# A scratch copy of w1 in bf16, and w2 loaded behind the first FFN1 stretch

## The chip, the cores and the metric

One Trainium2 chip, all 8 cores. Every core runs the same program on its own 2048 rows of x (with 128 rows of neighbours on either side), and holds all weights. The time is that of the slowest core, in microseconds (us). Before the change it is 1194.36 us, the median of 2 runs (1194.09 and 1194.64).

## What is computed

The input is x of shape (4, 4096, 1024). It is normalised per row, goes through an attention whose weights are fixed Gaussians, and beside it through a feed-forward net; both results are added to x.

```python
xn = _layernorm(x, axis=-1)
# attention: 8 heads of 128 columns
v = xn @ input_weights.T
attended = einsum('hqk,bhkd->bhqd', gaussian_probs, v)
att = attended @ output_weight.T
# feed-forward: w1 is 1024 x 4096, w2 is 4096 x 1024
h = relu(einsum('bsd,dw->bsw', xn, w1) + b1)
ffn = einsum('bsw,wd->bsd', h, w2) + b2
return x + att + ffn
```

The Gaussians are narrow (a deviation of at most 8 rows), so a block of 128 rows needs three blocks of v.

## The kernel before

The program is written out instruction by instruction for five engines through a small class, `Emitter`. `op` appends an instruction to one engine's list, with the events it waits for, and returns an event: a semaphore and a value. The DMAs of GpSimd all raise the semaphore `w` by 16, those of SyncE raise `x` and `o`. Since DMAs of one semaphore can land out of order, `op` groups them: GpSimd may issue `BATCH` = 4 DMAs, then the next one first waits until all those so far have landed (a drain), and the event of each DMA in a group gets the count of the whole group as its value. So whoever waits for one DMA of a group waits for all of it.

In order of the program:

- *Start.* SyncE loads b1, b2 and the identity. GpSimd loads win (L158), wout (L161) and w2 in four quarters (L166); all are f32 in HBM and are cast to bf16 by the DMA. VectorE and ScalarE make the 24 blocks of Gaussian weights (`probsT`; L193 writes each). Then TensorE transposes win and wout in 128 blocks (L206), and VectorE copies them out of PSUM (L211).
- *Half H = 0 and 1*, each 1024 rows of the result. Layer norm of 10 tiles of 128 rows, mostly on VectorE, with 8 transposes a tile on TensorE (L283). The product with win, 160 matmuls (L308). The Gaussian blocks, 192 small matmuls (L333).
- *Quarter Q = 0 and 1 of each half*, 512 rows. FFN1: 32 chunks `wc` of 128 columns of w1. GpSimd loads a chunk into one of four buffers `w1b` (L361), TensorE does 8 matmuls of 128x512 (L373), ScalarE applies bias and relu and writes h (L381). A buffer is free again when the matmuls of the chunk four earlier are done. Two neighbouring chunks, an even and the odd one behind it, share a PSUM tile, and the odd one waits for the relu of the even one. FFN2 (L418): 4 tiles, each 16 matmuls with wout and 64 with w2 into one PSUM tile; VectorE adds x and b2 (L423, L425); SyncE stores. The first matmul of every tile waits for all relus and for the last load of w2.

So FFN1 comes four times, and w1 is read from HBM in f32 each time, in rows of 128 elements (512 B), 1024 such rows a chunk. `w1b` holds four chunks of 256 KB.

The order on GpSimd is that of the source: win, wout, four quarters of w2, then the chunks of w1, 32 in each of four stretches. With six DMAs ahead of the chunks, a group begins at chunk 2, 6, 10 and so on, and the group that begins at chunk 30 takes in chunks 0 and 1 of the next stretch.

## Time and profile before

| what | us |
|---|---|
| median of 2 runs | 1194.36 |
| profiled execution, its own time | 1198.85 |
| its span, slowest core (core 1) | 1197.3 |
| spans of the 8 cores | 1171.0 to 1197.3 |
| TensorE matmul busy | 713.8 (60% of the span) |
| VectorE, ScalarE busy | 183.2 and 154.4 |

The span is the time from the first to the last instruction of one core. The profiled execution is a single one; its own time is 4.5 us above the median. The profile gives each instruction a line of the kernel, its engine, what it wrote and read, and what released the engine when it had stood idle. TensorE has a granted clock with two levels, 2.4 GHz (1.0 in the profile) and 1.2 GHz (0.5); a stretch shows their mean.

### The profile page before, as it was taken

To read this page: it belongs to the slowest core of one execution; us is meant where nothing else is said; L and a number is where in the kernel's file an instruction comes from. 1 tells how busy PE (TensorE), PEld (TensorE's weight loads), DVE (VectorE), ACT (ScalarE), POOL (GpSimd) and SP (SyncE) were. 2 spreads that over 40 slices of the span, in tenths; PEclk is the share of its full clock that TensorE was granted. 3 is DMA by queue.
4 is the path that set the end of the run, shared out by engine and by line. 5 is a ranking of instruction groups with operands and counts; after the bars stand their busy time and mean duration, and the time that the engine had idled before them with its cause. 6 is when DMAs were issued, how large, how long until landed. Compare 5 with 4: busy or idle time off the path is not lost.

```text
span 1197.3 us, 9338 instructions; the slowest of 8 cores (1171.0 to 1197.3 us)
## 1 busy us (share of the span) xinstructions
PE 713.8 (60%) x3296; PEld 311.8 (26%) x3296; DVE 183.2 (15%) x460; ACT 154.4 (13%) x289; POOL 117.7 (10%) x139
## 2 busy tenths in 40 slices
PE   0041197546469954555995117944556995655898
PEld 0030145112124411121442103611112442211343
DVE  3165631000001100000012663200000110000011
ACT  3202103111110011111000220311111001111100
POOL 1010000121110011221000000012111001212000
PEclk9985589687789986776998558978777998777999
DMA  9996201475651255666212120057465016657111
GB/s 158 175 150 117 71 1 13 40 70 49 57 53 36 71 73 51 63 55 58 53 36 90 68 75 14 1 53 70 45 62 53 36 71 83 58 53 70 18 71 53
DMA packets 147325, 74.58 MB, mean 62 GB/s; under 512 B 134352, under 2 KB 134352, under 8 KB 147280
## 3 DMA queue, kind: packets, MB, share of 16 engines
q0 software_dynamic: 139360, 46.15, 37.6%
q1 hardware_dynamic: 7920, 27.84, 6.6%
q8 instruction: 28, 0.46, 0.2%
q14 instruction: 17, 0.14, 0.0%
HBM read 111.72 MB, written 8.39 MB: 100 GB/s over the span
## 4 chain that ended last, share of the span: by engine, by line
PE 59%; DMA 16%; issue 7%; DVE 5%; another core or an unknown queue 5%; ACT 4%; DVEq 3%; ACTq 0%; POOL 0%; POOLq 0%; SPq 0%
PE pd L373 25%; PE pd L418 23%; DMA w1b<-w 14%; PE pd L308 6%; ACT arena L381 4%; DVEq L67 3%; PE pd L333 2%; DMA xsl<-xp 2%; PE ptr L283 1%; DVE xntm L274 1%; PE ptr L206 1%; DVE stat L270 0%; DVE stat L266 0%; DVE stat L262 0%
## 5 line engine op out<-in xcount | busy, mean ns | idle before, releaser
L373 PE MATMUL pd<-xn_fm,w1b 128*128 128x512 bf16 x1024 | 310.4, 463 | 268.1 <-DMA w1b<-w 205.3
L373 PEld LDWEIGHTS pd<-xn_fm,w1b 128*128 128x128 bf16 x1024 | 108.3, 112 | 469.0 <-issue 406.3
L418 PE MATMUL pd<-w_sb,arena 128*128 128x512 bf16 x1024 | 223.6, 379 | 0.0
L361 POOL DMA_DIRECT2D w1b<-w x128 | 111.9, 875 | 938.1 <-PE pd L373 861.8
L381 ACT ACTIVATE arena<-pd,b_sb 128x512 bf16<-128x512 f32 x128 | 88.2, 689 | 631.0 <-PE pd L373 631.0
L425 DVE SCALAR_TENSOR_TENSOR xsl<-pd,xsl 128x1024 f32<-128x1024 f32 x16 | 19.6, 1225 | 749.0 <-PE pd L418 749.0
L418 PEld LDWEIGHTS pd<-w_sb,arena 128*128 128x128 bf16 x1024 | 100.2, 98 | 120.8
L283 PE MATMUL ptr<-id_sb,xntm 128*128 128x128 bf16 x160 | 20.2, 306 | 139.6 <-DVE xntm L274 139.6
L308 PE MATMUL pd<-wintT,xn_fm 128*128 128x512 bf16 x320 | 73.5, 394 | 0.0
L418 PE MATMUL pd<-woutT,arena 128*128 128x512 bf16 x256 | 57.9, 379 | 4.7 <-ACT arena L381 4.7
L283 PEld LDWEIGHTS ptr<-id_sb,xntm 128*128 128x128 bf16 x160 | 15.5, 137 | 144.5 <-issue 144.5
L206 PE MATMUL ptr<-id_sb,arena 128*128 128x128 bf16 x128 | 11.7, 253 | 63.6 <-DMA w_sb<-w 61.8
L308 PEld LDWEIGHTS pd<-wintT,xn_fm 128*128 128x128 bf16 x320 | 32.4, 101 | 40.4 <-issue 5.5
L423 DVE TENSOR_TENSOR xsl<-xr,b_sb 128x1024 f32<-128x1024 f32 x16 | 19.6, 1224 | 96.6 <-DMA xr<-xp 96.6
L418 PEld LDWEIGHTS pd<-woutT,arena 128*128 128x128 bf16 x256 | 24.8, 98 | 36.1 <-issue 6.9
L240 ACT ACTIVATE xr<-xsl 128x1024 f32<-128x1024 f32 x20 | 21.1, 1057 | 90.5 <-DMA xsl<-xp 88.3
L314 DVE CAST arena<-pd 128x1024 bf16<-128x1024 f32 x20 | 24.5, 1225 | 49.7 <-PE pd L308 49.7
L206 PEld LDWEIGHTS ptr<-id_sb,arena 128*128 128x128 bf16 x128 | 9.4, 114 | 65.7 <-issue 65.5
L237 DVE TENSOR_REDUCE stat<-xsl 128x1 f32<-128x1024 f32 x20 | 24.2, 1210 | 6.7 <-DMA xsl<-xp 6.7
L333 PE MATMUL pd<-probsT,arena 128*128 128x128 bf16 x384 | 21.8, 219 | 3.1 <-DVE arena L314 3.1
L333 PEld LDWEIGHTS pd<-probsT,arena 128*128 128x128 bf16 x384 | 21.5, 98 | 4.0 <-issue 4.0
L255 ACT ACTIVATE stat<-stat 128x1 f32<-128x1 f32 x20 | 4.1, 204 | 131.6 <-DVE stat L252 131.6
(31 smaller groups left out, 149.4 us busy)
## 6 DMA issues: line engine op xcount, KB each, us to landing
w1b<-w POOLq DMA_DIRECT2D x128, 256.0 KB, 5.0
xsl<-xp SPq DMA_DIRECT2D x20, 512.0 KB, 3.3
w_sb<-w POOLq DMA_DIRECT2D x4, 2048.0 KB, 37.9
xr<-xp SPq DMA_DIRECT2D x16, 512.0 KB, 3.3
out<-xsl SPq DMA_DIRECT2D x16, 512.0 KB, 2.7
arena<-win POOLq DMA_DIRECT2D x1, 2048.0 KB, 19.2
arena<-wout POOLq DMA_DIRECT2D x1, 2048.0 KB, 33.0
b_sb<-b2t SPq DMA_DIRECT2D x1, 512.0 KB, 10.3
```

The costliest lines, as they stand in the source:

```text
L67: eng.drain()
L206: lambda e, base=base, ic=ic, jc=jc, pslot=pslot: e.transpose(ptr[pslot][:, jc * 128:(jc + 1) * 128], arena[:, base + ic * 1024 + jc * 128 ...
L237: E.op(V, [ev_x[t]], lambda e, t=t: e.reduce_sum(stat[:, 4 * t:4 * t + 1], xsl[t % 2][:, :], axis=AX.X))
L240: ev_sq[(H, t)] = E.op(SC, sq_waits, lambda e, t=t: e.activation(xr[0][:, :], xsl[t % 2][:, :], AF.Square, accum_out=stat[:, 4 * t + 1:4 * ...
L283: lambda e, t=t, dc=dc: e.transpose(ptr[t % 2][:, dc * 128:(dc + 1) * 128], xn_tm[t % 2][:, dc * 128:(dc + 1) * 128], id_sb[:, :]),
L308: lambda e, t=t, jc=jc, gq=gq, pslot=pslot, first=first, last=last: e.matmul(pd[pslot][:, gq * 512:(gq + 1) * 512], xn_fm[:, jc * 1280 + t ...
L314: ev_vevac[t] = E.op(V, [ev_mm], lambda e, t=t, pslot=pslot: e.tensor_copy(arena[:, V0 + t * 1024: V0 + (t + 1) * 1024], pd[pslot][:, :]), ...
L333: lambda e, h=h, qt=qt, di=di, kv=kv, pslot=pslot, last=last: e.matmul(pd[pslot][:, qt * 128:(qt + 1) * 128], arena[:, V0 + kv * 1024 + h ...
L361: ev_w1[wc] = E.op(G, ww, lambda e, wc=wc: e.dma_start(w1buf[wc % 4][:, :].rearrange("p (c n) -> p c n", c=8), w1.rearrange("(c p) n -> p ...
L373: lambda e, wc=wc, dc=dc, Q=Q, pslot=pslot, sub=sub: e.matmul(pd[pslot][:, sub * 512:(sub + 1) * 512], w1buf[wc % 4][:, dc * 128:(dc + 1) ...
L381: ev_relu[wc] = E.op(SC, [ev], lambda e, wc=wc, pslot=pslot, sub=sub: e.activation(arena[:, H0C + wc * 512: H0C + (wc + 1) * 512], pd[pslo ...
L418: lambda e, statn=statn, movn=movn, gq=gq, pslot=pslot, first=first, last=last: e.matmul(pd[pslot][:, gq * 512:(gq + 1) * 512], statn(e), ...
```

## The change

There are two parts. First, a tensor `w1s` in HBM, of 32 chunks of 128 x 1024 in bf16, is added. In the first FFN1 stretch (H = 0, Q = 0) each chunk is loaded from w1 as before, and then stored from its buffer to `w1s`. The store is preceded by a new method `qdrain`, which makes GpSimd wait for all its DMAs so far and closes the group. The other three stretches load their chunks from `w1s`, without a cast, in 128 rows of 2 KB; each of these loads also waits for the event of its store. Second, the four quarters of w2 are no longer issued at the start but by `emit_w2_loads`, behind the 32 chunks of the first stretch and ahead of the first FFN2. A third edit names stretches of the program and issues nothing.

```diff
+    def qdrain(self, eng):
+        evs = [Ev(k, self.cnt[k]) for k in self.QUEUE_KEYS[eng] if self.cnt[k] > 0]
+        for pev in self.pending[eng]:
+            pev.val = self.cnt[pev.key]
+        self.pending[eng] = []
+        self.since_drain[eng] = 0
+        return evs
...
+    w1s = nc.dram_tensor("w1s", [32, 128, 1024], BF16, kind="Internal").ap()
...
-    ev_w2 = None
-    for i in range(4):
-        ev_w2 = E.op(G, [], lambda e, i=i: e.dma_start(
-            w2_sb[:, i * 8192:(i + 1) * 8192].rearrange("p (c n) -> p c n", c=8),
-            w2.rearrange("(c p) n -> p c n", p=128)[:, i * 8:(i + 1) * 8, :]), inc=("w", 16))
+    w2_state = {"ev": None}
+
+    def emit_w2_loads():
+        if w2_state["ev"] is not None:
+            return
+        for i in range(4):
+            w2_state["ev"] = E.op(G, [], lambda e, i=i: e.dma_start(
+                w2_sb[:, i * 8192:(i + 1) * 8192].rearrange("p (c n) -> p c n", c=8),
+                w2.rearrange("(c p) n -> p c n", p=128)[:, i * 8:(i + 1) * 8, :]), inc=("w", 16))
...
                 ww = take(f"w1b{bslot}")
-                ev_w1[wc] = E.op(G, ww, lambda e, wc=wc: e.dma_start(
-                    w1buf[wc % 4][:, :].rearrange("p (c n) -> p c n", c=8),
-                    w1.rearrange("(c p) n -> p c n", p=128)[:, :, wc * 128:(wc + 1) * 128]),
-                    inc=("w", 16))
+                if H == 0 and Q == 0:
+                    ev_w1[wc] = E.op(G, ww, lambda e, wc=wc: e.dma_start(
+                        w1buf[wc % 4][:, :].rearrange("p (c n) -> p c n", c=8),
+                        w1.rearrange("(c p) n -> p c n", p=128)[:, :, wc * 128:(wc + 1) * 128]),
+                        inc=("w", 16))
+                    ev_scr = E.op(G, E.qdrain(G), lambda e, wc=wc: e.dma_start(
+                        w1s[wc, :, :], w1buf[wc % 4][:, :]), inc=("w", 16))
+                    ev_w1scr[wc] = ev_scr
+                    use(f"w1b{bslot}", ev_scr)
+                else:
+                    ev_w1[wc] = E.op(G, ww + [ev_w1scr[wc]], lambda e, wc=wc: e.dma_start(
+                        w1buf[wc % 4][:, :], w1s[wc, :, :]), inc=("w", 16))
...
+            emit_w2_loads()
...
-                waits = [ev_relu[31], ev_att[7], ev_woutT_done, ev_w2] + take(f"pd{pslot}")
+                waits = [ev_relu[31], ev_att[7], ev_woutT_done, w2_state["ev"]] + take(f"pd{pslot}")
```

GpSimd from the iota at the start of the program, before the change (`arena` holds win and wout, `w_sb<-w` is w2, `w1b<-w` is w1; `sw` is the semaphore `w`, `st_` that of TensorE):

```order
L155 IOTA g_sb 128x128
L158 DMA arena<-win 128x8x1024
L161 DMA arena<-wout 128x8x1024
L166 DMA w_sb<-w 128x8x1024 x2
L166 DMA w_sb<-w 128x8x1024 [waits sw]
L166 DMA w_sb<-w 128x8x1024
L361 DMA w1b<-w 128x8x128 x2
L361 DMA w1b<-w 128x8x128 [waits sw]
L361 DMA w1b<-w 128x8x128
L361 DMA w1b<-w 128x8x128 [waits st_] x2
L361 DMA w1b<-w 128x8x128 [waits st_,sw]
L361 DMA w1b<-w 128x8x128 [waits st_] x3
```

The last two rows repeat to the end of the program: one load in four waits for the queue. The same place after the change:

```order
L166 IOTA g_sb 128x128
L169 DMA arena<-win 128x8x1024
L172 DMA arena<-wout 128x8x1024
L382 DMA w1b<-w 128x8x128
L386 DMA w1s<-w1b 128x1024 [waits sw]
```

w2 is gone from there, the first group holds three DMAs, and behind it load and store take turns, each store with a wait for the queue; from the fifth chunk on a load also waits for TensorE and for the store of its buffer. GpSimd at the end of the first FFN1 stretch after the change:

```order
L382 DMA w1b<-w 128x8x128 [waits sw,st_]
L386 DMA w1s<-w1b 128x1024 [waits sw]
L181 DMA w_sb<-w 128x8x1024 x3
L181 DMA w_sb<-w 128x8x1024 [waits sw]
L391 DMA w1b<-w1s 128x1024 [waits sw,st_] x4
L391 DMA w1b<-w1s 128x1024 [waits st_,sw] x92
L479 UNCONDITIONAL_BRANCH
```

The last store and three quarters of w2 are one group; the fourth quarter and chunks 0, 1 and 2 of the next stretch are the next, so that later groups begin at chunks 3, 7, 11 and so on to 31. All 96 loads from `w1s` show a wait for `sw` here, since each also names its store's event; every fourth of them is a drain. TensorE's order is the same before and after.

## Rows read from the trace of the kernel before

**Rows 1.** The chain that ended last, share of the span by line.

```profile
PE pd L373 25%; PE pd L418 23%; DMA w1b<-w 14%; PE pd L308 6%; ACT arena L381 4%; DVEq L67 3%; PE pd L333 2%; DMA xsl<-xp 2%; PE ptr L283 1%; DVE xntm L274 1%; PE ptr L206 1%; DVE stat L270 0%; DVE stat L266 0%; DVE stat L262 0%
```

**Rows 2.** Costliest groups: line, engine, out<-in, count | busy, mean ns | idle before, releaser.

```profile
L373 PE MATMUL pd<-xn_fm,w1b 128*128 128x512 bf16 x1024 | 310.4, 463 | 268.1 <-DMA w1b<-w 205.3
...
L361 POOL DMA_DIRECT2D w1b<-w x128 | 111.9, 875 | 938.1 <-PE pd L373 861.8
```

**Rows 3.** Waits: engine, line, for whom: us in total, times, longest us.

```profile
PE pd L373 <- DMA w1b<-w: 205.3, 32, 9.7
...
POOL w1b L361 <- issue: 42.4, 7, 9.1
```

**Rows 4.** Timeline of TensorE, fourth FFN1: start, us, instruction [idle before <-releaser].

```profile
992.69 1.89 PE L373 MATMUL pd<-xn_fm,w1b 128*128 128x512 bf16 x8 [1.48 <-DVE xsl L425]
...
1003.08 3.57 PE L373 MATMUL pd<-xn_fm,w1b 128*128 128x512 bf16 x8 [5.69 <-DMA w1b<-w]
1007.59 3.61 PE L373 MATMUL pd<-xn_fm,w1b 128*128 128x512 bf16 x16 [0.93 <-ACT arena L381]
...
1019.82 3.57 PE L373 MATMUL pd<-xn_fm,w1b 128*128 128x512 bf16 x8 [5.81 <-DMA w1b<-w]
```

**Rows 5.** Four FFN1 stretches: us, busy of PE, PEld, DVE, ACT, POOL, PEclk, DMA share, GB/s.

```profile
200.95:352.11 151.16, 76.88 (x259) 27.00 (x257) 0.00 (x0) 22.82 (x34) 27.77 (x32) 0.75 0.59 54
422.82:574.39 151.57, 82.64 (x256) 28.27 (x257) 1.23 (x1) 22.05 (x32) 27.68 (x32) 0.73 0.61 61
775.39:921.98 146.59, 76.54 (x259) 26.70 (x257) 0.00 (x0) 22.81 (x34) 27.11 (x31) 0.77 0.59 55
992.69:1123.55 130.86, 74.30 (x257) 26.23 (x257) 1.23 (x1) 22.06 (x32) 24.48 (x28) 0.79 0.62 64
```

**Rows 6.** Timeline of GpSimd and of SyncE's queue at the start.

```profile
1.60 1.01 POOL L158 DMA_DIRECT2D arena<-win  x1 [0.29 <-issue]
...
2.97 0.33 SPq L152 DMA_DIRECT2D b_sb<-b2t  x1
...
3.48 1.76 POOL L166 DMA_DIRECT2D w_sb<-w  x2
...
62.07 1.76 POOL L166 DMA_DIRECT2D w_sb<-w  x2 [56.83 <-DMA w_sb<-w]
```

**Rows 7.** Timeline of TensorE, its first instructions.

```profile
61.78 6.56 PE L206 MATMUL ptr<-id_sb,arena 128*128 128x128 bf16 x56 [61.78 <-DMA w_sb<-w]
```

**Rows 8.** Timeline of VectorE, from the last of the Gaussian weights.

```profile
42.40 0.29 DVE L193 SCALAR_TENSOR_TENSOR probsT<-e_sb,pm_sb 128x128 bf16<-128x128 f32 x1
62.90 0.69 DVE L211 COPY wintT<-ptr 128x1024 bf16<-128x1024 bf16 x1 [20.21 <-PE ptr L206]
```

**Rows 9.** The chain in order of time around the last load: start, us, what.

```profile
1112.45 0.02 issue
...
1112.98 4.34 DMA w1b<-w
1117.32 0.35 issue
```

**Rows 10.** DMA queues (packets, MB, share of 16 engines), issues (count, KB each, us to landing).

```profile
q0 software_dynamic: 139360, 46.15, 37.6%
q1 hardware_dynamic: 7920, 27.84, 6.6%
...
w1b<-w POOLq DMA_DIRECT2D x128, 256.0 KB, 5.0
xsl<-xp SPq DMA_DIRECT2D x20, 512.0 KB, 3.3
...
out<-xsl SPq DMA_DIRECT2D x16, 512.0 KB, 2.7
```

**Rows 11.** The chain in order of time, from 222 to 236 us.

```profile
225.48 4.14 issue
```

**Rows 12.** DMA queues between 30 and 60 us.

```profile
q0 software_dynamic: 2338, 4.71, 100.2%
```

**Rows 13.** DMA queues between 1017 and 1036 us.

```profile
q0 software_dynamic: 5077, 1.28, 71.8%
```

More of the change, by code:

```diff
@@ L43, in __init__ @@
         self.since_drain = {k: 0 for k in self.ops}
+        self.phase = "init"
     def op(self, eng, waits, build, inc=None, drain=False):
@@ L76, in closure @@
                 inst.then_inc(closure.sems[_inc[0]], _inc[1])
+        closure.phase = self.phase
         self.ops[eng].append(closure)
         return ev
+    def qdrain(self, eng):
[5 more added lines that the diff above has]
+        return evs
     def finalize(self):
@@ L220, in build_nc @@
         E.op(SY, [ev_winT_done], lambda e: e.dma_start(d_wint[:, :], wintT[:, :]), inc=("o", 16))
+    ev_w1scr = {}
     ev_apply = {}
@@ L227, in build_nc @@
     for H in range(2):
+        E.phase = f"ln{H}"
         ev_x = {}
@@ L296, in build_nc @@
             E.op(SY, [ev_pdevac[9]], lambda e: e.dma_start(d_stat[:, :], stat[:, :]), inc=("o", 16))
+        E.phase = f"vproj{H}"
         ev_vevac = {}
@@ L321, in build_nc @@
                 d_v[:, :], arena[:, V0:V0 + 10240]), inc=("o", 16))
+        E.phase = f"conv{H}"
         ev_att = {}
@@ L352, in build_nc @@
         for Q in range(2):
+            E.phase = f"ffn1_{H}{Q}"
             ev_w1 = {}
@@ L392, in build_nc @@
                     d_h[:, :], arena[:, H0C:H0C + 16384]), inc=("o", 16))
+            E.phase = f"ffn2_{H}{Q}"
+            emit_w2_loads()
             ev_xr = {}
@@ L459, in run_all @@
             def run_all(eng, ops=ops):
+                import contextlib
+                cur = None
+                stk = contextlib.ExitStack()
                 for c in ops:
+                    if c.phase != cur:
+                        stk.close()
+                        stk = contextlib.ExitStack()
+                        stk.enter_context(nc.named_scope(c.phase))
+                        cur = c.phase
                     c(eng)
+                stk.close()
             attr(run_all)
```

## Prediction

> **What bounds the kernel now.** I read the chain that ended last first [rows 1]: by line, the matmuls of FFN1 (L373) and FFN2 (L418) are 25% and 23% of the span, and the w1 loads come next with 14%, as a thing that TensorE waits for. The groups by line say where TensorE stands idle [rows 2]: before the FFN1 matmuls of L373, 268.1 us. The waits name what ended them [rows 3]: 205.3 us are 32 waits for `w1b<-w`, 6.4 in the mean, eight in each of the four stretches of FFN1.
>
> The timeline of one round of four chunks [rows 4] shows why there are eight. The GpSimd queue issues four DMAs, waits until all have landed, and a chunk's event stands for its whole group. So TensorE waits for the last of four loads, and that one waits for a buffer that TensorE frees last. In row order: 3.57 us for the first 8 matmuls after the wait, at half the clock, a gap of 0.93 for ScalarE's relu, 16 matmuls in 3.61, a gap again, 8 in 1.89 (the first row has such a group), and 5.8 of idling: 16.74 us a round. The stretches of FFN1 took 151.16, 151.57, 146.59 and 130.86 us [rows 5], with a granted clock of 0.73 to 0.79. The other stretch without TensorE is the start: its first instruction begins at 61.78 [rows 7].
>
> **The change, part by part.** All sums go against the profiled execution (1198.85 us; its span is 1197.3).
>
> *The start.* GpSimd issued win, wout and two quarters of w2 as one group, so the transposes waited for 8.39 MB of bf16 [rows 6, 7]. Now the group is win, wout and one w1 chunk, 4.46 MB: at the DMA rate below (13.4 us for 2.10 MB) that is 28.5 us, with 4.5 for 1.6 MB of x and b2 at the rate of SyncE's queue, and issued at 1.6 with 1.8 fixed it lands at about 37. VectorE, which must copy each transpose out, is busy with the probabilities until 42.69 and then sat idle for 20.21 us [rows 8]. So the first copy moves from 62.90 to about 42.7, VectorE becomes the bound, and all that follows moves with it. **-20.2.** If the group lands at 45 instead, it is -18.
>
> *FFN1 of half 0, quarter 0, which now fills the scratch.* Each chunk's store drains the queue, and so each load of w1 starts only after the load before it has landed and the store has been issued. A lone load takes 4.34 us from issue to landing, and GpSimd goes on 0.53 after what released it, from 1112.45 to 1112.98 [rows 9]; an issue costs 0.875 [rows 2]. So the period is 0.53 + 0.875 + 4.34 = 5.75 us. The store's own landing lies beside the next load. Its nearest row, out stores of 512 KB, lands in 2.7 [rows 10]. TensorE needs 3.57 a chunk even at the lower clock, which is less than 5.75: it is no longer the bound. Four chunks are there already; the load of chunk 4 is issued at 1.89+0.53 = 2.4, that of chunk 31 27 periods later, at 157.7, it lands at 162.0, and after its store (0.53+0.875) the first load of w2 is issued at 163.4. The period's ends are 5.2 (if a store of 128 rows costs as little as SyncE's issue of 0.33, rows 6) and 6.6 (loads at the median of 5.0, rows 10, and a little more).
>
> To this come pauses. GpSimd stops now and then although it waits for nothing: once for 4.14 us [rows 11], and seven times in all, 42.4 us with the waits around them [rows 3]. There are 128 loads with one wait each, or two at the start of a group, so 288 instructions and one pause in 41. The filling stretch has 5 a chunk, 160 in all, so four pauses. In a serial chain they count; I take 2.75 each, +11 (ends 0 and 18).
>
> *w2, moved behind it.* `emit_w2_loads` stands behind the 32 chunks on GpSimd, and TensorE's FFN2 waits for it with nothing else to do: there is no cover. Between 30 and 60 us the queue moved 4.71 MB in 30 us [rows 12], so 13.4 us for a quarter of 2.10 MB. Three quarters go together: 1.8 fixed (worked out below) + 40.2 = 42.0. Then comes the drain, 0.53, and the fourth quarter goes in a group with three scratch loads, whose landing FFN2 must await too: 1.8 + 13.4 + 3 x 0.74 = 17.4. With 0.35 for TensorE to start this makes 60.3 (ends 54 and 66; the first four transfers of before took until 61.54). FFN2 starts at 163.4 + 11 + 60.3 = 234.7 after FFN1's first matmul, and it did at 151.2. After such a wait it begins at half the clock, 1.68 us for the first 8 matmuls [rows 4] and something for the next: +2. **+85.5.**
>
> *The three other stretches of FFN1.* A load from scratch is 128 rows of 2 KB without a cast, not 1024 pieces of 512 B. What that saves follows from SyncE's queue, which moved 27.84 MB in 6.6% of the span, 2.84 us per MB, 0.74 for a chunk [rows 10]; a 512 KB load of x takes 1.49 at that rate and lands in 3.3, so 1.8 is fixed. The landing is thus 2.6. Ends are 2.3 and the 3.3 of the transfer twice as large. The stall becomes 0.53 + 2.6 + 0.35 = 3.5 (3.2 to 4.2) instead of 6.4 in the mean. The Trainium skill, DMA: Bandwidth & Descriptors, on the anatomy of one DMA, gives 2.0 us plus the bytes at 436 GB/s: an estimate of 2.6 for this chunk, which agrees, but by the same fit a w1 load would land in 2.6 too, where this trace has 4.34.
>
> The groups also shift. Before, a group began at chunk 2 of every four; in the new order one w2 quarter and chunks 0 to 2 form a group, and groups begin at 3, 7, ... 31. The stall now lies between an even chunk and the odd one behind it, just where the relu gap was, and swallows it. A round is 3.5 + 3.61 + 0.93 + 3.61 = 11.65 and the clock. After each stall the first 8 matmuls took 1.68 more than at the full clock, and often the next ones too; 3.5 us of idling has no row, its neighbours are 1.48 (no fall, rows 4) and 5.7 (always a fall). I take 1.6 a round (ends 0 and 2.6), so 13.25. Two stretches of 8 rounds are 106 each; the last has 7 and four chunks without a stall (8.2): 101. With 3 instructions a load now, 288 in all, there are seven pauses, of which only a delayed last load counts: +13 together (ends 4 and 20). So 326 instead of 151.57+146.59+130.86 = 429. **-103.**
>
> **Sum:** -20.2 + 85.5 - 103 = -37.7, from 1198.85 to 1161.2; the median of before is 4.5 below its profiled run, so 1157.
>
> **Rivals.** (a) *The store becomes the bound of the filling stretch.* The drain ahead of each store also waits for the store before. Were a load held up until that store has landed, the 2.7 of rows 10 would come on top of each of the 27 periods: +73, so 1230, slower. It decides from a period of 8.0 on. Against it: both are in flight together and the store has a lead of 0.875.
> The Trainium skill, DMA: Bandwidth & Descriptors, on the anatomy of one DMA, warns that a completion is held back until the last byte's write is confirmed, longest for a target in HBM; no row here shows a GpSimd write to HBM, and this is what would make (a) true.
> (b) *Scratch loads land no sooner*, because the time lies in the queue and not in the small pieces: the stall stays at 5.7, +2.2 and +0.8 of clock on 23 rounds, +69, so 1226, slower. Against it: four loads in flight fill the DMA engines (71.8% of a stretch of 19 us went into 5077 packets; 139360 packets for 134 loads are 1040 each; so 2.8 us of all 16 engines a load) [rows 10, 13], and 4.34 less 2.8 leaves 1.5 for the rest.
> (c) *The clock holds through 3.5 us of idling* (-37), or the pauses hide behind waits (-24): 1120 or 1133.
> (d) The exposed w2 and the filling stretch each reach their upper ends: 0.85 x 27 + 7 + 6 = +36, so 1193, within 2%.
>
> **Chances.** Forecast 0.60, (a) 0.07, (b) 0.07, (c) 0.13, (d) 0.13. The forecast's own spread crosses the 2% bound (1170.5; about what a measurement of this kernel can tell) with a sixth of its weight; a part of (a) and (b) ends milder, within 2%. This makes faster 0.67, same 0.23, slower 0.10. The range 1120 to 1195 takes in (c) and (d), and leaves out (a) and (b) and the far end of (c).
>
> **What would show it.** Right: the first wintT copy at about 43; issues of w1 5.75 us apart in the filling stretch, with TensorE idle for most of it and at the lower clock; one wait of about 60 us ahead of FFN2 of the first quarter; 23 waits for `w1b<-w1s` of 3.5 us, with two relu gaps a round turned into one. Wrong: waits for scratch above 5 us, a period above 7, or a wait for w2 of much less than 50, which would mean that its rate was set by something else at the start.

## The result, and the profile after

The changed kernel takes 1163.0 us (median of 11 runs) against 1196.72 for the kernel before (10 runs beside them): a ratio of 0.972, with an interval of 0.969 to 0.975. It is 2.8% faster. The slowest core of the profiled execution, core 4, has a span of 1161.4 us; against the 1197.3 of before this is 35.9 less, 2 more than the medians differ by, since the profiled execution of before was itself 2 us above its median here.

The chain that ended last, share of the span by line; it answers to [rows 1]:

```profile
PE pd L448 24%; PE pd L401 19%; DMA w1b<-w 11%; DMA w1b<-w1s 7%; PE pd L326 6%; DMA w_sb<-w 4%; DVEq L68 3%; PE pd L352 2%; PE ptr L300 2%; ACT arena L409 2%; DVE xntm L291 1%; ACT e_sb L203 1%; ACT t_sb L201 1%; DVE stat L287 1%; DVE stat L283 1%
```

FFN1 is now L401, FFN2 L448. FFN1's matmuls fell from 25% of the chain to 19%, but the loads as a whole did not become small: 11% for w1, though only one stretch of four still reads it, 7% for the scratch, and w2 is new with 4%. The groups, as in [rows 2] (count, busy, mean ns of one, idle before):

```profile
L401 PE MATMUL pd<-xn_fm,w1b 128*128 128x512 bf16 x1002 | 304.0, 464 | 196.2 <-DMA w1b<-w1s 89.8
L391 POOL DMA_DIRECT2D w1b<-w1s x96 | 51.6, 539 | 633.0 <-PE pd L401 532.4
L382 POOL DMA_DIRECT2D w1b<-w x32 | 28.5, 890 | 127.9 <-PE pd L401 125.1
L386 POOL DMA_DIRECT2D w1s<-w1b x32 | 18.4, 575 | 171.9 <-DMA w1b<-w 171.9
```

The DMA issues, as in [rows 10] (count, KB each, median us from issue to landing):

```profile
w1b<-w1s POOLq DMA_DIRECT2D x96, 256.0 KB, 2.9
...
w1b<-w POOLq DMA_DIRECT2D x32, 256.0 KB, 4.6
w1s<-w1b POOLq DMA_DIRECT2D x32, 256.0 KB, 2.3
```

Idling ahead of FFN1's matmuls fell from 268.1 to 196.2. The mean of one matmul is unchanged (464 ns): a mean over a filling stretch that runs slower than before and three that run faster. TensorE's waits, as in [rows 3], and the two of GpSimd that concern the store and the pauses (a pause is idle time for which the profile shows nothing that was waited for, `issue`); in us total, times, longest:

```profile
POOL w1s L386 <- DMA w1b<-w: 171.9, 32, 36.6
...
PE pd L401 <- DMA w1b<-w1s: 89.8, 23, 4.5
...
PE pd L401 <- DMA w1b<-w: 75.8, 27, 5.3
...
PE pd L448 <- DMA w1b<-w1s: 59.7, 1, 59.7
...
PE pd L401 <- ACT arena L409: 25.6, 27, 1.2
...
POOL w1b L391 <- issue: 7.1, 1, 7.1
```

32 waits of 6.4 us have become three kinds: 23 of 3.9 for the scratch, 27 of 2.8 in the filling stretch, and one of 59.7 for w2. Where the time went is a matter of stretches. The table of windows, in order the filling stretch up to its last matmuls, the wait for w2, and the three stretches from the scratch (us; busy of PE, PEld, DVE, ACT, POOL; granted clock; DMA share; GB/s). It answers to [rows 5]:

```profile
179.60:351.95 172.35, 94.02 (x250) 29.36 (x254) 0.00 (x0) 21.89 (x32) 42.77 (x59) 0.66 0.58 86
351.95:411.62 59.67, 0.00 (x1) 0.03 (x1) 0.00 (x0) 0.69 (x1) 3.19 (x5) 0.50 0.93 154
483.93:595.33 111.40, 70.69 (x252) 27.05 (x258) 1.23 (x1) 21.99 (x32) 17.20 (x32) 0.86 0.28 83
798.31:909.53 111.22, 71.14 (x251) 27.05 (x255) 0.00 (x0) 22.58 (x33) 17.19 (x32) 0.86 0.25 73
982.05:1087.63 105.58, 68.11 (x251) 26.35 (x257) 1.22 (x1) 21.99 (x32) 15.04 (x28) 0.89 0.27 80
```

From FFN1's first matmul to FFN2's the first quarter now takes 232.0 us (before 151.2), the other three 328.2 (before 429.0). The sum of the parts:

| part | before | after | difference |
|---|---|---|---|
| start of the first FFN1 | 200.95 | 179.60 | -21.35 |
| first FFN1 to its FFN2 | 151.16 | 232.02 | +80.9 |
| FFN2 after w2, first 16 matmuls 5.22 instead of 3.61 | | | +1.6 |
| three other stretches of FFN1 | 429.02 | 328.20 | -100.8 |
| FFN2 of two quarters, first 16 matmuls 5.52 and 5.43 instead of 3.61 | | | +3.7 |
| sum | | | -35.95 |

It is the 35.9 of the spans. The -100.8 of the three stretches is the big gain, and four fifths of it is paid away by the +80.9 of the first. TensorE's timeline shows a piece of each (start, us, instruction, idle before and what ended it); the rows from 509.57 answer to [rows 4]:

```profile
40.67 1.86 PE L221 MATMUL ptr<-id_sb,arena 128*128 128x128 bf16 x16 [40.67 <-DMA w1b<-w]
...
206.24 3.16 PE L401 MATMUL pd<-xn_fm,w1b 128*128 128x512 bf16 x8 [2.48 <-DMA w1b<-w]
212.10 1.89 PE L401 MATMUL pd<-xn_fm,w1b 128*128 128x512 bf16 x8 [2.70 <-DMA w1b<-w]
...
411.62 5.22 PE L448 MATMUL pd<-woutT,arena 128*128 128x512 bf16 x16 [59.67 <-DMA w1b<-w1s]
...
509.57 5.30 PE L401 MATMUL pd<-xn_fm,w1b 128*128 128x512 bf16 x16 [3.97 <-DMA w1b<-w1s]
515.80 3.61 PE L401 MATMUL pd<-xn_fm,w1b 128*128 128x512 bf16 x15 [0.93 <-ACT arena L409]
523.20 5.30 PE L401 MATMUL pd<-xn_fm,w1b 128*128 128x512 bf16 x16 [3.79 <-DMA w1b<-w1s]
...
595.33 5.52 PE L448 MATMUL pd<-woutT,arena 128*128 128x512 bf16 x16 [1.14 <-ACT arena L409]
```

TensorE starts at 40.67 instead of 61.78 [rows 7], and VectorE's first copy of wintT follows its last probabilities with nothing between (before [rows 8]):

```profile
42.20 1.28 DVE L226 COPY wintT<-ptr 128x1024 bf16<-128x1024 bf16 x2
```

In the filling stretch TensorE gets 8 matmuls every 5.8 us. In a round from the scratch there is one wait, 16 matmuls in 5.30 (at the full clock they take 3.61), one relu gap (the 0.93 that an odd chunk waits for the relu of the even one), and 16 in 3.61: 13.63 us a round. It was 16.74 in the rows of the fourth stretch [rows 4], the shortest of the four before. GpSimd's timeline beside it shows what paces the filling stretch, and how w2 stands at its end:

```profile
206.45 0.57 POOL L386 DMA_DIRECT2D w1s<-w1b  x1 [4.24 <-DMA w1b<-w]
207.02 0.89 POOL L382 DMA_DIRECT2D w1b<-w  x1
212.22 0.57 POOL L386 DMA_DIRECT2D w1s<-w1b  x1 [4.31 <-DMA w1b<-w]
...
233.18 0.89 POOL L382 DMA_DIRECT2D w1b<-w  x1 [2.57 <-PE pd L401]
...
310.02 0.88 POOL L382 DMA_DIRECT2D w1b<-w  x1 [2.45 <-issue]
...
349.97 2.64 POOL L181 DMA_DIRECT2D w_sb<-w  x3
392.97 0.88 POOL L181 DMA_DIRECT2D w_sb<-w  x1 [40.36 <-DMA w_sb<-w]
```

Store and load take turns. The idle time ahead of the store is the load's landing, the chain is closed, and between these rows nothing else of TensorE's or GpSimd's is in it. At 310.02 one of the pauses stands in the row of a load. The 2.57 at 233.18 is put down to TensorE, but the buffer's matmuls had long been done by then (they ended by 214), so it is taken as a pause too. The fourth quarter of w2 goes out only when the first three have landed, 40.4 us later.

### The profile page after: what moved, and what is told of

Same layout as the page of the kernel before. It is cut to its first block, busy times and chain, and to the rows that moved or that the text cites. A ratio compares the mean times of both kernels' runs of the same rounds, so it can differ in the third digit from the quotient of the medians.

```text
span 1161.4 us, 9438 instructions; the slowest of 8 cores (1150.2 to 1161.4 us)
## 1 busy us (share of the span) xinstructions
PE 710.6 (61%) x3240; PEld 314.8 (27%) x3296; DVE 182.0 (16%) x460; ACT 153.9 (13%) x289; POOL 104.1 (9%) x171
## 3 DMA queue, kind: packets, MB, share of 16 engines
q0 software_dynamic: 49760, 54.54, 24.4%
## 4 chain that ended last, share of the span: by engine, by line
PE 53%; DMA 22%; issue 9%; DVE 7%; ACT 4%; DVEq 4%; POOL 0%; ACTq 0%; POOLq 0%; SPq 0%
PE pd L448 24%; PE pd L401 19%; DMA w1b<-w 11%; DMA w1b<-w1s 7%; PE pd L326 6%; DMA w_sb<-w 4%; DVEq L68 3%; PE pd L352 2%; PE ptr L300 2%; ACT arena L409 2%; DVE xntm L291 1%; ACT e_sb L203 1%; ACT t_sb L201 1%; DVE stat L287 1%; DVE stat L283 1%
## 5 line engine op out<-in xcount | busy, mean ns | idle before, releaser
L401 PE MATMUL pd<-xn_fm,w1b 128*128 128x512 bf16 x1002 | 304.0, 464 | 196.2 <-DMA w1b<-w1s 89.8
L448 PE MATMUL pd<-w_sb,arena 128*128 128x512 bf16 x1004 | 222.6, 379 | 1.1
L401 PEld LDWEIGHTS pd<-xn_fm,w1b 128*128 128x128 bf16 x1024 | 110.1, 113 | 388.3 <-issue 322.2
L448 PEld LDWEIGHTS pd<-w_sb,arena 128*128 128x128 bf16 x1024 | 100.2, 98 | 120.8
L391 POOL DMA_DIRECT2D w1b<-w1s x96 | 51.6, 539 | 633.0 <-PE pd L401 532.4
L300 PE MATMUL ptr<-id_sb,xntm 128*128 128x128 bf16 x160 | 20.2, 307 | 138.8 <-DVE xntm L291 138.8
L448 PE MATMUL pd<-woutT,arena 128*128 128x512 bf16 x250 | 62.9, 404 | 63.4 <-DMA w1b<-w1s 59.7
L448 PEld LDWEIGHTS pd<-woutT,arena 128*128 128x128 bf16 x256 | 26.1, 103 | 99.5 <-issue 73.3
L326 PEld LDWEIGHTS pd<-wintT,xn_fm 128*128 128x128 bf16 x320 | 32.4, 101 | 40.4 <-issue 5.5
L382 POOL DMA_DIRECT2D w1b<-w x32 | 28.5, 890 | 127.9 <-PE pd L401 125.1
L386 POOL DMA_DIRECT2D w1s<-w1b x32 | 18.4, 575 | 171.9 <-DMA w1b<-w 171.9
```

Of the source, the lines that this page charges most:

```text
L300: lambda e, t=t, dc=dc: e.transpose(ptr[t % 2][:, dc * 128:(dc + 1) * 128], xn_tm[t % 2][:, dc * 128:(dc + 1) * 128], id_sb[:, :]),
L326: lambda e, t=t, jc=jc, gq=gq, pslot=pslot, first=first, last=last: e.matmul(pd[pslot][:, gq * 512:(gq + 1) * 512], xn_fm[:, jc * 1280 + t ...
L382: ev_w1[wc] = E.op(G, ww, lambda e, wc=wc: e.dma_start(w1buf[wc % 4][:, :].rearrange("p (c n) -> p c n", c=8), w1.rearrange("(c p) n -> p ...
L391: ev_w1[wc] = E.op(G, ww + [ev_w1scr[wc]], lambda e, wc=wc: e.dma_start(w1buf[wc % 4][:, :], w1s[wc, :, :]), inc=("w", 16))
L401: lambda e, wc=wc, dc=dc, Q=Q, pslot=pslot, sub=sub: e.matmul(pd[pslot][:, sub * 512:(sub + 1) * 512], w1buf[wc % 4][:, dc * 128:(dc + 1) ...
L448: lambda e, statn=statn, movn=movn, gq=gq, pslot=pslot, first=first, last=last: e.matmul(pd[pslot][:, gq * 512:(gq + 1) * 512], statn(e), ...
```

## The experiments

All times are medians, and all ratios are against the kernel before, run on the same chip beside them (1196.4, 1201.6 and 1191.8 us in three batches, the experiments in the order in which they stand here: four, four, four). The changed kernel was not run again beside them, and the kernel before differs by up to 10 us between the batches; so a step to the changed kernel's 1163.0, or between experiments of two batches, is sure to some 10 us only, and where it is small the stretches of the traces are given too. The texts written ahead of the runs call the experiments by other names: e1 to e5 are 1 to 5 here, e7, e8 and e9 are 6, 7 and 8, e11 is 9, e10 is 10, e12 is 11 and e13 is 12. The short diffs are against the changed kernel unless said otherwise.

The theory was that of the prediction: three independent parts, of which w2 behind the filling stretch costs some 60, and the scratch gives some 103 and costs the filling of some 25.

**1. w2 issued behind chunk 3, not behind chunk 31.**

```diff
                     use(f"w1b{bslot}", ev_scr)
+                    if wc == 3:
+                        emit_w2_loads()
```

> The four w2 quarters move on GpSimd to just behind the store of chunk 3, so they run during the layer norm, when the DMA engines were nearly idle. Theory (w2 is fully exposed ahead of the first FFN2, 59.7 us of waiting, and nothing else depends on its place): the wait is gone, the gain at the start stays, 1163 - 60 = about 1103. Rival (the w2 traffic shifts the trouble: tiles of x land late and the layer norm stretches, or chunk 4 comes late): 1125 or more, with VectorE waiting for x between 60 and 125 us.

Measured: 1108.6 us, ratio 0.930 (0.926 to 0.934). w2 now loads beside the layer norms of the first half. FFN2 of the first quarter begins like this, with no wait for w2 at all:

```profile
355.09 5.64 PE L450 MATMUL pd<-woutT,arena 128*128 128x512 bf16 x16 [1.23 <-DMA w1b<-w1s]
```

The x tiles land in 4.2 us instead of 3.4 while w2 is moving, and FFN1 begins 3.5 us later (183.06). So the place of w2 in this change costs 54 us, about what was predicted for it, and it is pure loss: two lines take it back.

**2. w2 at the very start, as before, and the scratch kept.**

```diff
+    emit_w2_loads()
```

directly behind its definition.

> w2 is issued at the start as in the kernel before, all else as in the changed kernel. Theory (start worth 20.7, w2 wait worth 59.7 and 1.6 of clock): the first copy of wintT is back at about 63, 1163 + 20.7 - 61 = about 1123. Rival (the moved w2 costs less than its wait, since FFN2 would have waited for something else): 1145 or more.

Measured: 1125.4 us, ratio 0.943 (0.940 to 0.946). TensorE's first instruction is back at 63.2 and FFN2 does not wait for w2. It is 17 us slower than the first experiment, whose earlier start gives 22 and whose slower x tiles take 3.5 back. Both halves of the w2 edit are thus priced: the start gives 22, the position behind the stretch takes 60 when it is exposed.

**3. Only w2 moved, no scratch.** All four stretches load w1 with the cast, and the stores are gone. Two DMAs stand ahead of the chunks, so the groups begin at chunks 2, 6, ... again.

```diff
-                if H == 0 and Q == 0:
+                if True:
...
-                    ev_scr = E.op(G, E.qdrain(G), lambda e, wc=wc: e.dma_start(
-                        w1s[wc, :, :], w1buf[wc % 4][:, :]), inc=("w", 16))
```

> Only w2 is moved; all four FFN1 stretches load from w1 in f32 as in the kernel before, no stores. Theory: start -20.7, w2 exposed by about 60 ahead of the first FFN2, the rest as before: 1196 - 21 + 61 = about 1236. So the scratch alone must be worth about -73 on top of this. Rival (the moved w2 is nearly free and the scratch brings little): 1180 to 1200.

Measured: 1216.7 us, ratio 1.020 (1.016 to 1.023). That is 19 us less than expected, 24 by the traces. The timeline of TensorE around the end of the first stretch tells where 13 of them are:

```profile
347.91 3.25 PE L394 MATMUL pd<-xn_fm,w1b 128*128 128x512 bf16 x8 [30.22 <-DMA w_sb<-w]
...
379.58 6.20 PE L441 MATMUL pd<-woutT,arena 128*128 128x512 bf16 x16 [25.59 <-DMA w1b<-w]
```

The exposed w2 comes in two pieces. Chunk 30 was in one group with two quarters of w2 and waits 30.2 us for them; FFN2 waits 25.6 for the rest. The first piece stands where an ordinary wait of 6.5 would have stood, so the first quarter took 199.4 us from FFN1 to FFN2, 48 more than before and not 61. Another 14 are in the three other stretches, 414.9 us instead of 429.0 with the same loads in the same groups; no row tells why. FFN2's start at half the clock (6.20 instead of 3.61) takes 3 back. From here to the changed kernel it is 54 us, but that step is two things at once, the scratch and the shift of the groups by one chunk; the next experiment parts them.

**4. The drains put back to an even chunk.** In the change the groups begin at chunk 3, 7, ..., by the count of DMAs ahead. One more is counted, and they begin at 2, 6, ..., as before the change.

```diff
             emit_w2_loads()
+            if H == 0 and Q == 0:
+                E.since_drain[G] += 1
```

> The changed kernel, but one group of GpSimd's DMAs is closed one DMA earlier behind w2, so that groups begin at chunks 2, 6, ... 30 again instead of 3, 7, ... 31. Theory (the shift let the wait swallow a relu gap of 0.93 in each round and let 16 matmuls follow it): three relu gaps or 2 in a round instead of 1, 0.9 to 1.4 us more in each of 23 rounds, 1163 + 21 to 32 = 1184 to 1195. Rival (only the landing time matters): 1163 within 5.

Measured: 1233.7 us, ratio 1.034 (1.031 to 1.037): 70 us over the changed kernel, twice the largest loss that I had allowed, and slower than the kernel before. Neither theory held it. The waits are not longer:

```profile
PE pd L401 <- DMA w1b<-w1s: 90.0, 23, 4.4
...
PE pd L401 <- ACT arena L409: 46.7, 50, 1.2
```

90.0 us against 89.8, and 23 more relu gaps, 21 us. The other 49 are in the matmuls. One round in TensorE's timeline:

```profile
508.48 3.57 PE L401 MATMUL pd<-xn_fm,w1b 128*128 128x512 bf16 x8 [3.96 <-DMA w1b<-w1s]
512.98 5.71 PE L401 MATMUL pd<-xn_fm,w1b 128*128 128x512 bf16 x16 [0.93 <-ACT arena L409]
519.62 1.89 PE L401 MATMUL pd<-xn_fm,w1b 128*128 128x512 bf16 x8 [0.93 <-ACT arena L409]
525.31 3.57 PE L401 MATMUL pd<-xn_fm,w1b 128*128 128x512 bf16 x8 [3.81 <-DMA w1b<-w1s]
```

Behind the wait the first 8 matmuls take 3.57 (at the full clock 8 take 1.89, as in the third row), then comes a relu gap, and then 16 more take 5.71 instead of 3.61. The clock costs 1.68 + 2.10 = 3.8 a round, where the changed kernel pays 1.69. With the gap of 0.93 that is 3.1 a round and 72 in 23 rounds. The granted clock of the first such stretch fell from 0.86 to 0.71:

```profile
483.07:619.91 136.84, 88.78 (x256) 29.41 (x257) 1.22 (x1) 21.98 (x32) 17.21 (x32) 0.71 0.23 68
```

So in this order of gaps and waits the clock costs more than twice the gap's own length on top of it. Experiments 9 and 10 test this. It is no rule for every gap behind a wait, though: the kernel before has the same two gaps at the same places, and its rows go both ways. In the fourth stretch the 16 matmuls take 3.61 [rows 4], in the second they can look like this:

```profile
454.50 3.57 PE L373 MATMUL pd<-xn_fm,w1b 128*128 128x512 bf16 x8 [6.75 <-DMA w1b<-w]
459.00 5.97 PE L373 MATMUL pd<-xn_fm,w1b 128*128 128x512 bf16 x16 [0.93 <-ACT arena L381]
```

Over its four stretches the 16 were slow (5.2 to 6.0) in 10 rounds of 28, behind waits of 5.3 to 9.7 us. Here, behind waits of 3.8 to 4.4, they were slow (5.3 to 5.9) in 21 of 21. The matmuls of the three later stretches were busy for 262.5 us, and for 233.5 in the kernel before [rows 5]: at the same place of the groups the waits became shorter and the matmuls, by the clock, took 29 us longer. So this kernel, scratch and all, is 17 us slower than experiment 3, which has none (its three stretches are only 14 us shorter, 400.8 against 414.9, and its first is 31 longer).

**5. Pieces of 256 B in the scratch.** The scratch is laid out like w1, 1024 rows of 128 elements a chunk, so that the loads keep their 1024 small pieces and lose only the cast (and with it the f32 bytes).

```diff
-    w1s = nc.dram_tensor("w1s", [32, 128, 1024], BF16, kind="Internal").ap()
+    w1s = nc.dram_tensor("w1s", [32, 1024, 128], BF16, kind="Internal").ap()
...
-                        w1buf[wc % 4][:, :], w1s[wc, :, :]), inc=("w", 16))
+                        w1buf[wc % 4][:, :].rearrange("p (c n) -> p c n", c=8),
+                        w1s[wc, :, :].rearrange("(c p) n -> p c n", p=128)), inc=("w", 16))
```

(and the store in the same way).

> The changed kernel, but the scratch keeps each chunk as 1024 rows of 128 elements in bf16 (256 B) and is stored and loaded so: no cast, but as many pieces as a load of w1 has. Theory (a w1 load is slow for its 1024 pieces): scratch loads land in 4.3 us or more and queue up behind each other, the waits of the three later FFN1 stretches go from 3.9 back to 5.5 to 6.5 each, 23 of them, +37 to 60 and more through the clock, 1200 to 1240; the stores get slower too. Rival (the cast or the f32 bytes are what made it slow): waits stay at 3.9, 1163 within 10.

Measured: 1209.3 us, ratio 1.010 (1.001 to 1.020). The DMA issues (count, KB, us to landing), and TensorE's waits for them:

```profile
w1b<-w1s POOLq DMA_DIRECT2D x96, 256.0 KB, 3.5
w1b<-w POOLq DMA_DIRECT2D x32, 256.0 KB, 5.2
w1s<-w1b POOLq DMA_DIRECT2D x32, 256.0 KB, 3.3
```

```profile
PE pd L403 <- DMA w1b<-w1s: 105.7, 23, 6.9
```

A scratch load lands in 3.5, between the 2.9 of the rows of 2 KB and the 4.6 of w1, and TensorE waits 4.6 a time instead of 3.9. By the traces, 24 us are in the filling stretch (256.4 instead of 232.0 up to FFN2), where the store costs 0.90 to issue instead of 0.575 and a load of w1, itself unchanged, lands in 5.2 instead of 4.6, beside a store that now takes 3.3 instead of 2.3. The other 23 are in the three later stretches (351.2 instead of 328.2): 16 of longer waits, the rest by the clock (granted 0.84 to 0.86 instead of 0.86 to 0.89). The small pieces are thus worth 0.6 of a landing, half of it perhaps the longer issue (0.88 instead of 0.54), and the larger rest, 1.1, belongs to what is special in the load from w1: the cast, its packets, twice the bytes read, and rows that lie 16 KB apart in HBM where a scratch chunk is one block. These cannot be told apart by this run, because the pieces did not stay pieces and these four went at once. DMA queue in 540 to 600 us, first of the changed kernel (17 loads), then of this one (16):

```profile
q0 software_dynamic: 1360, 4.46, 26.2%
```

```profile
q0 software_dynamic: 1280, 4.20, 24.1%
```

Both have 80 packets a load; the load with the cast had 1040 [rows 10]. So neither theory is shown in full. The time lies in the first one's 1200 to 1240, but the waits (4.6, not 5.5 to 6.5) do not, and half of the loss is where it had put no number.

**6. The store issued by SyncE.** The first experiment, and the store goes to the other queue, waits there for its chunk's event (which stands for the group of four) and for SyncE's DMA before it, and needs no drain on GpSimd, whose loads of w1 go in groups of four again. A drain ahead of the last quarter of w2 keeps the groups at chunks 3, 7, ....

```diff
-                    ev_scr = E.op(G, E.qdrain(G), lambda e, wc=wc: e.dma_start(
-                        w1s[wc, :, :], w1buf[wc % 4][:, :]), inc=("w", 16))
+                    ev_scr = E.op(SY, [ev_w1[wc]], lambda e, wc=wc: e.dma_start(
+                        w1s[wc, :, :], w1buf[wc % 4][:, :]), inc=("x", 16))
...
+                    if wc == 3:
+                        emit_w2_loads()
...
+            if i == 3:
+                E.since_drain[G] = 4
```

> w2 behind chunk 3 as in e1, and the 32 stores to the scratch are issued by SyncE, each after its chunk has landed; GpSimd's w1 loads are in groups of four again, beginning at chunks 3, 7, ... Theory (the drain ahead of each store makes the filling stretch a serial chain of 5.7 us a chunk, 172 us in all): without it a round of four takes 17 to 18.6 us (a wait of 6, or the four stores of 3.3 us each that now hold the buffers), 136 to 149 us, so 1109 - 23 to 36 = 1073 to 1086. Rival (the writes to HBM or the DMA engines bound the stretch, whoever issues them): no gain over e1, 1109 within 8.

Measured: 1074.3 us, ratio 0.895 (0.890 to 0.901). The filling stretch takes 142.9 us up to FFN2, where the first experiment took 172.0 (and the kernel before 151.2, without storing anything). So what cost 29 us was the serial chain of load and store on one queue, not the traffic of the stores, which is still there. They are not without a price: GpSimd waits 11 times, 66.7 us in all, for a store that still holds the buffer of its next load.

**7. Groups of two for the scratch loads.** Only the size of a group is changed, behind the filling stretch.

```diff
             emit_w2_loads()
+            E.BATCH = {"sync": 1, "gpsimd": 2}
```

> The changed kernel, but from the second FFN1 stretch on GpSimd's groups hold two DMAs instead of four. Theory (what is left of each wait, 3.9 us, is one landing that lies in the open only because TensorE must finish all four buffers of a group first): two chunks load while two are multiplied, 4.5 us of work cover 3.9 of landing, the waits go to nearly nothing, and with them the falls of the clock; a stretch takes 16 x 4.54 = 73 us instead of 106 to 111, so 1163 - 112 = about 1050. Rival (the added drains and shorter groups cost as much as they hide, a wait of 2 us at every second chunk with the clock still falling): 1120 or more.

Measured: 1055.4 us, ratio 0.880 (0.874 to 0.886), 108 us under the changed kernel by one line. With two groups of two in four buffers, one group lands while TensorE uses the other, and a landing of 3.0, with 0.5 to issue it and 0.5 to react, fits in the 4.5 us of two chunks. The windows of the three stretches:

```profile
483.61:557.88 74.27, 57.55 (x252) 23.83 (x257) 1.22 (x1) 21.99 (x32) 16.71 (x31) 1.00 0.41 125
760.29:834.69 74.40, 57.34 (x251) 23.72 (x256) 0.00 (x0) 22.59 (x33) 16.71 (x31) 1.00 0.37 110
905.39:979.38 73.99, 57.55 (x252) 23.80 (x258) 1.23 (x1) 21.99 (x32) 15.09 (x28) 1.00 0.37 114
```

74.2 us each instead of 109.4 in the mean. The clock is 1.00: no wait, no half clock. What TensorE still idles there are the relu gaps.

**8. Experiments 1, 6 and 7 together.**

> All three together: w2 behind chunk 3, stores by SyncE, groups of two from the second FFN1 stretch on. Theory: the terms add, since each lies in a stretch of its own: e7's time less 112, 960 to 975. Rival (they share a cover): 1000 or more.

Measured: 965.4 us, ratio 0.802 (0.797 to 0.808). From the changed kernel's 1163.0 the sum of the steps would be 54 (w2) + 34 (SyncE) + 108 (groups) = 196 off, 967. They add up, as closely as batches can be compared.

**9. The changed kernel without the relu gap inside a PSUM tile.** An odd chunk writes its own half of the tile and need not wait for the relu of the even one. The wait for the relu four chunks earlier, which wrote to the same half, stays, and so does the one for the tiles at a stretch's start.

```diff
-                waits = [ev_w1[wc], ev_b1] + take(f"ph{bslot}") + take(f"pd{pslot}")
+                waits = [ev_w1[wc], ev_b1] + take(f"ph{bslot}")
+                if wc in (0, 2):
+                    waits = waits + take(f"pd{pslot}")
```

> The changed kernel without relu gaps, groups at chunk 3. Theory: a round loses its one gap of 0.93 and no clock, 13.6 to 12.7, 1163 - 21 = about 1142, level with e10. Rival: 1163 within 5, if the matmuls that follow then wait for something else (the relu of four chunks earlier, ScalarE).

Measured: 1151.5 us, ratio 0.966 (0.962 to 0.971). 11.5 us less, where the gaps amount to 25.6. That is hardly more than batches differ by, but the trace shows it too: the four FFN1 stretches take 546.0 us instead of 560.2. In the timeline the 32 matmuls of a round are now one group:

```profile
515.89 9.72 PE L403 MATMUL pd<-xn_fm,w1b 128*128 128x512 bf16 x32 [3.84 <-DMA w1b<-w1s]
```

At the full clock they take 7.07 (experiment 11 has such a row, at 180.70), so the clock costs 2.65 a round and not 1.69. The round is 13.7 us, as before the edit: in the middle of a stretch the gap was given back whole by the clock. What was gained lies at the start of each scratch stretch, where the first two rounds behind a wait take 12.1 and 12.6 us, and, 3.6 us of it, in the filling stretch.

**10. The same with the groups at chunks 2, 6, ... (experiments 4 and 9 together).**

> As e4 (groups begin at chunk 2), but TensorE waits for the tile pd only at chunks 0 and 2 of a stretch; the wait for the relu four chunks earlier stays, so no relu gap is left. Theory, formed after e4 (the relu gap right behind the first 8 matmuls after a wait is what keeps the clock low for another 16, and that made e4 70 us slower than the changed kernel): a round is 3.9 of waiting, 7.1 of matmuls and 1.7 to 2.0 of clock, 12.9 instead of 17.05, so 1234 - 23 x 4.2 = about 1137, and the same as e11 within 10. Rival (the place of the group alone costs the 70 us, through the loads): e10 stays 50 us or more above e11.

Measured: 1154.6 us, ratio 0.969 (0.966 to 0.972). The same place in its timeline:

```profile
518.12 9.95 PE L403 MATMUL pd<-xn_fm,w1b 128*128 128x512 bf16 x32 [3.55 <-DMA w1b<-w1s]
```

With the gap the place of the groups made 70 us, without it 3 (both of these runs are of one batch). So it is not where the drain stands as such, nor the DMA behind it, that cost 70 in experiment 4. It is the relu gaps as that order places them: one 8 matmuls behind the wait, the other 8 ahead of the next. This run takes out both, and which of them does it was not tested; that the first does is my reading, since the slow matmuls stand right behind it. Both runs without gaps are slower than their theories (1137 and 1142), which had put the clock at 1.7 to 2.0 a round: it costs 2.65 in experiment 9 and 2.9 here.

**11. Everything: experiments 8 and 9.**

> e9 without relu gaps. Theory: in the three scratch stretches two chunks now take 3.5 us of matmuls, and the landing of 3.9 is no longer covered: 0.93 a pair is saved and 0.4 to 0.6 comes back as a wait, 48 pairs, -16 to -25, and some 8 more in the first stretch: 965 - 24 to 33 = 932 to 941. Rival (short waits at each pair let the clock fall): 965 or more.

Measured: 943.5 us, ratio 0.792 (0.790 to 0.794), the best version: 21% under the kernel before. Without the gaps TensorE takes a group of two sooner than it lands, and 31 waits of 0.7 us come back (21.4 in all, against 3.7 in experiment 8); that is what keeps the step at 22 (by the traces 19.5, 362.8 us of FFN1 to 343.3).

**12. The kernel before, with nothing but its groups shifted to chunks 3, 7, ....** (Diff against the kernel before.)

```diff
     for i in range(4):
+        if i == 3:
+            E.since_drain[G] = 4
```

> The kernel before with one thing changed: a group is closed ahead of the last w2 quarter, so that groups begin at chunks 3, 7, ... 31 in all four stretches. No scratch, w2 at the start. Theory (the place of the wait is worth about as much as the scratch): the gap behind the wait is gone, 0.93 a round and part of the clock (2.4 us a round in the mean before, 1.7 after), 31 rounds, -50 to -35, so 1196 - 35 to 50 = 1146 to 1161. Rival (with waits of 6 us the clock's share does not change and the gain is the gap alone or nothing): 1167 to 1196.

Measured: 1179.0 us (10 runs), ratio 0.991 (0.987 to 0.995): under 1%, and not the 1146 to 1161 of my theory. Its waits in the profile:

```profile
PE pd L375 <- DMA w1b<-w: 233.7, 31, 11.4
PE pd L375 <- ACT arena L383: 31.4, 33, 1.2
```

The relu gaps went down as expected, from 59.9 us to 31.4. But the waits for w1 went up by as much, from 205.3 to 233.7 [rows 3] (the profiled execution is 10 us over the median of its runs, so some of this is its own), and a w1 load's landing from 5.0 to 5.7. The four stretches take 568.3 us instead of 580.2. Waits and gaps cancel, so these 12 are the matmuls' own time, at a granted clock of 0.77 to 0.80 instead of 0.73 to 0.79. With loads as long as these, a gap that is swallowed is mostly waited for again.

## Why the prediction was right

It said 1157 us, in a range of 1120 to 1195; it was 1163.0. The difference was predicted as -37.7 against the profiled execution, and came as -35.9. The terms:

- *Start, predicted -20.2, was -21.35.* The first copy of wintT begins at 42.20, at once behind the last probabilities (predicted 42.7). TensorE's first transpose was there at 40.67, so VectorE is what bounds it. Right in size and mechanism. The landing at 37 was some 3 us too early, which didn't matter, as VectorE was later in any case.
- *Filling stretch.* FFN2 was to begin 234.7 after FFN1, and began 232.0 after. The period came out, 5.77 between the two stores of the rows above against 5.75, but by two errors that cancel: the store's issue is 0.575 and not the 0.875 taken, and the load lands in 4.6 and not 4.34. The pauses came to about 5.4 us and not 11 (0.33, 2.57 and 2.45 are what the timeline shows; the middle one it puts down to TensorE). The first load of w2 went out 170.4 after FFN1's start; 163.4 + 11 = 174.4 was predicted. The clock was granted at 0.66 in the stretch and cost nothing, as said.
- *w2, predicted 60.3, was 61.65* from its first issue to FFN2, 59.67 of them as TensorE's one wait. The groups were 43.0 and 18.65 (17.4 and 0.35 predicted for the second). Experiment 1 confirms by its -54 that it is exposed, and that little else was hidden behind it.
- *The three other stretches, predicted 326, were 328.2.* The nearness is partly luck. A scratch load lands in 2.9, not in 2.6, so a wait is 3.9 and not 3.5: +0.4 in 23 rounds, +9. By this row the Trainium skill's fit (DMA: Bandwidth & Descriptors, on the anatomy of one DMA), an estimate of 2.6, comes out 0.3 too short, as my own did. The clock came out at 1.69 a round, 1.6 predicted; the prediction had no row for it and said so. A round is 3.84 + 5.30 + 0.93 + 3.61 = 13.7, 13.25 predicted. But the 13 us of pauses did not come: TensorE waits 23 times for 3.9 with nothing above 4.5, and the one pause that GpSimd's waits list (7.1) fell where it was waiting anyway. Some 6 more come at the ends of the stretches (in each of the first two one relu gap of 1.2 that the sum had left out, and 5.9 and 6.6 instead of 5.30 behind the first wait). So +9, +6 and -13 cancel.
- *The reason given for that gain was only half of it.* The prediction had the wait swallow the relu gap, worth 0.93 a round. Experiment 4 shows that the same shift is worth 3.1 a round, because in the shifted order the clock comes back 8 matmuls sooner. The sum was right since its clock term, 1.6, was guessed and happened to fit the shifted order; that is luck. Nor do scratch and shift simply add up: with the groups at an even chunk the scratch makes the kernel 17 us slower (experiment 3 to 4), with the groups at an odd chunk some 54 faster (experiment 12 to 2, w2 at the start in both), and the shift alone gives 13 (experiment 12). Had I been asked what the change gives without the shift, I would have said about 1190, and it is 1234, slower than before. The change's 2.8% hang on a count of DMAs that puts the groups at an odd chunk.
- *Not foreseen:* two FFN2 begin at half the clock (5.52 and 5.43 instead of 3.61), since the last wait now stands in front of the last chunk and not of the last but one. +3.7.

The rivals. (a), the store as the bound: it lands in 2.3 us, beside the next load, and the period stayed at 5.8. Refuted; the Trainium skill's warning (same page, same section) that a write to HBM is confirmed late would have made it true, and this store's 2.3 doesn't bear it out. (b), scratch loads no faster: 2.9 against 4.6; refuted. Experiment 5 shows that its reasoning had something in it, though: small pieces are the lesser part of the gain. (c), two halves: the clock did not hold through 3.9 us of idling; the pauses mostly did not show, which gave 13 + 6 of the 24. (d), both upper ends: not reached.

What stays open: how much of a w1 load's 4.6 us is the cast, how much its 1040 packets, its f32 bytes or the 16 KB between its rows (experiment 5 removed all of them at once); what decides how long the clock stays low behind a wait, since the same gaps cost more behind 3.9 us than behind 5.3 to 9.7; and why the pauses are so much fewer in the changed kernel (42.4 us in seven waits before, 9.9 in three now), though GpSimd issues more instructions.

## What to carry to other kernels

When a transfer is moved to make the start earlier, look for the last place where it is still hidden, not for the place right before its use: issued 28 chunks earlier w2 was nearly free (FFN1 began 3.5 us later), and there the change gives 7% and not 2.8%. When a counter groups DMAs, count the groups against the buffers: four buffers in one group of four are no double buffer, and groups of two were worth 108 us, three times what the change gave as a whole. And read what stands right behind a wait: a gap that TensorE meets soon after it has idled can cost three times its length, and a shorter wait need not be a gain until the rows behind it have been read.

## What the runs showed of the hardware

- *The clock after a wait depends on the order of gaps around it.* The same waits of 3.9 us cost 1.69 us of clock a round with 16 matmuls in a row on either side of one gap, 3.8 with gaps of 0.93 behind the first 8 and ahead of the last 8, and 2.65 with 32 in a row. The same two gaps with waits of 5.3 to 9.7 us (the kernel before) kept the 16 matmuls between them slow in 10 rounds of 28, with waits of 3.8 to 4.4 (experiment 4) in 21 of 21. Idle time removed within a round is not always time won: experiment 9 left the round at 13.7. Without any waits the clock is 1.00 through a whole stretch with 0.93 of gap at every second chunk (experiment 7), and with waits of 0.7 us in the mean as well (experiment 11).
- *Packets.* A load of 1024 rows with a cast took 1040 packets, whether of 256 KB or of 2 MB; the changed kernel's 49760 are 38 of those and 128 of 80. Without the cast 1024 rows of 256 B took 80, as did 128 rows of 2 KB.
- *Issue on GpSimd.* 0.89 us for a load of w1 (1024 rows with cast), 0.88 and 0.90 for 1024 rows without, 0.54 and 0.575 for 128 rows. The rows count, the cast does not.
- *A store of 256 KB from GpSimd to HBM* landed in 2.3 us, sooner than a load of the same size.
